# TensorE's attention batches as an engine loop, with the wait for the masked states ahead of the last head

## The chip, the cores and the metric

The kernel runs on one core of one Trainium2 chip. The time is the device time of one execution in microseconds; before the change it is 619.74 us, the median of three runs (619.48 to 620.28). Lower is better. Engines are named as in the profile: PE (TensorE), DVE (VectorE), ACT (ScalarE), POOL (GpSimd), SP (SyncE, which only issues transfers here).

## What is computed

A block of three sublayers on x of shape 8 x 512 x 128, all in float32:

```
x = x + 0.5 * ffn(layernorm(x))      # mixture of 64 experts, 6 per token, 64 slots each, and a shared expert
x = x + attention(layernorm(x))      # causal linear attention, 16 heads of 8
x = x + 0.5 * ffn(layernorm(x))

# attention, per batch and head, with feature map phi(z) = elu(z) + 1.0001:
q, k, v = split(x @ W_qkv + b_qkv);  q = phi(q / sqrt(8));  k = phi(k)
for t in range(512):
    kv += outer(k[t], v[t]);  ks += k[t]
    out[t] = (q[t] @ kv) / (q[t] . ks + 1e-6)
out @ W_out + b_out
```

## The kernel before

Each engine has one stream of instructions, written out by hand: the order in the source is the order of execution, and engines wait for each other with semaphores. The first feed-forward layer, the attention and the second feed-forward layer follow one another in every stream.

The attention goes batch by batch, one call of `step(b, par)` for each of the 8 batches; `par` is the parity of the batch and chooses between two buffers for q and v. The 512 tokens of a batch are cut into 4 groups q of 128, and these into 4 chunks of 32. Within a chunk, the scores are computed and masked; between chunks, a running state of key-value products is used. In PE's `step`:

- `project(b + 1)` (L835, L836, L838) computes q, k and v of the next batch: two matmuls with 512 columns and four with 128.
- `turn_out(b - 1)` (L856) transposes the output of the batch before.
- L880 is 64 score matmuls of 32 x 32 weights, in four groups of heads g. Between the groups come the state matmuls L899, 60 in all. After a wait for DVE's masking of a bank, the fourth group of states takes the first's bank again.
- `project_out(b - 1)` (L863) multiplies the transposed output by W_out.
- L913 is the score-value product: 16 heads h, 4 matmuls each. It waits for POOL's block-diagonal v (`vx_ready`) and for DVE's four masked scores (`sc_sb`, L1171).
- L926 is the product of q with the states, 60 matmuls. It waits for DVE's masked states (`kv_sb`, L1178) and their running sums (`sb_ready`, L1186). Its last one releases DVE's division (L1198) and POOL's L481 of the next batch (`o_ps`).
- `turn_k(b + 1)` (L848) transposes the next batch's k.

Each of these float32 products in L880, L899, L913, L926, L835, L836, L838 and L863 stands in the trace as two matmuls (128 for 64), each with a weight load (PEld); transposes stand as one. Waits are counts that grow with b, such as `PRIMED + NQ * (b + 1)`; no address depends on b beyond `par`.

DVE and POOL and, in its middle part, ACT already run their attention as loops of two steps (`Fori`), and their waits take values from a register. ACT's loop covers steps 1 to 4, DVE's steps 1 to 6. On PE the eight steps are written out: a Python loop emits steps 1 to 7 one after the other.

SP stores each batch's result and reads it back in another layout, when DVE has added the bias (L1159). The second feed-forward layer starts when that is back for the last batch.

Of the kernel before, what the change touches and what calls it, by code (L numbers as in the profile page):

```python
# [39 lines left out]
HEADS = 16  # L40
# [4 lines left out]
def macaron_kernel(nc, x, w_qkv, b_qkv, w_out, b_out, gate_wT, gate_b, w1T, w2T, w3T, ws1T, ws2T, ws3T, out):  # L45
    B, L, D = x.shape
# [9 lines left out]
    NQ = L // P  # L56
# [16 lines left out]
    with ctx:  # L73
# [3 lines left out]
        def sem(name):  # L77
            return ctx.enter_context(nc.semaphore(name))
# [155 lines left out]
        PRIMED = 1  # L234
# [18 lines left out]
        kv_sb = sem("kv_sb")  # L253
        sb_ready = sem("sb_ready")
# [413 lines left out]
        def _(pe):  # L668
# [158 lines left out]
            def project(b):  # L827

                pe.wait_ge(hTb_sb, b + 1)
                if not (isinstance(b, int) and b == 0):  # L830
                    pe.wait_ge(kv_sb, PRIMED + NQ * (b - 1))
                    pe.wait_ge(q_read, 2 * b)
                    pe.wait_ge(v_ready, b)
                    pe.wait_ge(k_read, 2 * b)
                pe.matmul(bank[0][:, :], wqkv[:, 0:D], HTB, start=True, stop=True).then_inc(qT_ps, 1)  # L835
                pe.matmul(bank[1][:, :], wqkv[:, D:2 * D], HTB, start=True, stop=True).then_inc(kT_ps, 1)  # L836
                for q in range(NQ):
                    ins = pe.matmul(bank[2][:, q * D:(q + 1) * D], HTB[:, q * P:(q + 1) * P], wqkv[:, 2 * D:3 * D],  # L838
                                    start=True, stop=True)
                ins.then_inc(v_ps, 1)  # L840

            def turn_k(b):

                if not (isinstance(b, int) and b == 0):
                    pe.wait_ge(oo_ready, PRIMED + b - 1)
                pe.wait_ge(k_ready, PRIMED + b + 1)
                for q in range(NQ):
                    ins = pe.transpose(bank[3][:, q * P:(q + 1) * P], KT[:, q * P:(q + 1) * P], ident[:, :])  # L848
                ins.then_inc(kn_ps, 1)

            def turn_out(b):
                if not (isinstance(b, int) and b == B - 1):
                    pe.wait_ge(kn_sb, PRIMED + NC * (b + 2))
                pe.wait_ge(an_ready, b + 1)
                for c in range(NC):
                    ins = pe.transpose(bank[3][:, c * P:(c + 1) * P], AN[:, c, :], ident[:, :])  # L856
                ins.then_inc(anT_ps, 1)

            def project_out(b):

                pe.wait_ge(anT_sb, b + 1)
                for c in range(NC):
                    ins = pe.matmul(bank[3][:, c * D:(c + 1) * D], AT[:, c * P:(c + 1) * P], wout[:, :],  # L863
                                    start=True, stop=True)
                ins.then_inc(pr_ps, 1)

            def step(b, par, first=False, last=False):
                if not last:
                    project(b + 1)
                pe.wait_ge(q4_ready, 4 * b + 4)  # L870
                pe.wait_ge(k_ready, PRIMED + b + 1)
                if not first:
                    turn_out(b - 1)

                for g in range(4):
                    rows = slice(32 * g, 32 * g + 32)
                    for q in range(NQ):
                        for c in range(NC):
                            t0 = q * P + c * CHUNK
                            ins = pe.matmul(bank[4 + g][CHUNK * c:CHUNK * c + CHUNK, q * P:(q + 1) * P]  # L880
                                            .rearrange("p (j t) -> p j t", j=4),
                                            KT[rows, t0:t0 + CHUNK], Q4[rows, :, t0:t0 + CHUNK],
                                            start=True, stop=True)
                    ins.then_inc(sc_ps, 1)

                    if g == 1:
                        pe.wait_ge(kn_sb, PRIMED + NC * (b + 1))
                        if last:
                            pe.wait_ge(v_ready, b + 1)
                        else:  # L890
                            pe.wait_ge(v_ready, b + 2)
                            pe.wait_ge(q_read, 2 * (b + 2))
                            pe.wait_ge(k_read, 2 * (b + 2))
                    for q in AFTER[g]:
                        if q >= len(STATES):
                            pe.wait_ge(kv_sb, PRIMED + NQ * b + q + 1 - len(STATES))
                        for c in range(NC if q < NQ - 1 else NC - 1):
                            for j in range(4):
                                ins = pe.matmul(bank[STATES[q % len(STATES)]][32 * j:32 * j + 32, c * GW:(c + 1) * GW],  # L899
                                                KN[:, c, q, 32 * j:32 * j + 32],  # L900
                                                VN[par][:, q, 4 * j:4 * j + 4, :].rearrange("p h f -> p (h f)"),
                                                start=True, stop=True)
                        ins.then_inc(kv_ps, 1)
                if not first:
                    project_out(b - 1)

                pe.wait_ge(vx_ready, PRIMED + NC * (b + 1))
                pe.wait_ge(sc_sb, 4 * b + 4)
                for h in range(HEADS):
                    ob = bank[4 + h // 4][:, 0:NC * GW].rearrange("p (c h f) -> p c h f", c=NC, h=4)  # L910
                    for q in range(NQ):
                        o = (h // 4) * L + q * P + (h % 4) * CHUNK
                        pe.matmul(ob[32 * q:32 * q + 32, :, h % 4, :], PR[:, o:o + CHUNK],  # L913
                                  VX[:, q, h, :, :], start=(h % 4 == 0), stop=False, skip_group_check=True)
                pe.wait_ge(kv_sb, PRIMED + NQ * (b + 1))
                pe.wait_ge(sb_ready, (NQ - 1) * (b + 1))
                for g in range(4):
                    rows = slice(32 * g, 32 * g + 32)
                    for c in range(NC):
                        for q in range(NQ):  # L920
                            if q + c == 0:
                                continue
                            t0 = q * P + c * CHUNK
                            before_c = SW[rows, q, c - 1, :] if c else SW[rows, q - 1, NC - 1, :]
                            o = c * GW
                            ins = pe.matmul(bank[4 + g][32 * q:32 * q + 32, o:o + GW], QT[par][rows, t0:t0 + CHUNK],  # L926
                                            before_c, start=False, stop=True, skip_group_check=True)
                ins.then_inc(o_ps, 1)
                if not last:
                    turn_k(b + 1)  # L930

            project(0)
            turn_k(0)
            step(0, 0, first=True)
            for b in range(1, B):
                step(b, b % 2, last=b == B - 1)
            turn_out(B - 1)
            project_out(B - 1)

# [315 lines left out]
```

## Time and profile before

| | |
|---|---|
| median of 3 runs | 619.74 us |
| the profiled execution | 623.67 us |
| its span, first to last instruction | 621.9 us |
| granted TensorE clock, mean | 0.698 |
| busy: PE, DVE, ACT, POOL | 441.1, 316.3, 237.2, 331.3 us |
| attention on PE, first projection to last | 236 to 396 us |
| steps 1 to 6 on PE | 264.6 to 372.6 us |

All times below come from the one profiled execution, 3.9 us above the median. A clock of 1.00 is 2.4 GHz, one of 0.50 is 1.2 GHz. "issue" as the releaser of a wait means that the profile shows nothing that the engine waited for: neither a semaphore of another engine nor a transfer. Idle time under 0.15 us is not listed as a wait. The queue whose kind is "instruction" carries the engines' own programs.

### The profile page before, as it was taken

Reading aid. Unit: us, or ns where it says so; the run is one execution under the profiler, and the core shown is the slowest. Engines: PE = TensorE matmul, PEld = TensorE weight load, DVE = VectorE, ACT = ScalarE, POOL = GpSimd, SP = SyncE. Lnnn points to the kernel's source line nnn. Section 1 sums busy time; section 2 is a strip of 40 time slices with the busy share of each in tenths; the row PEclk is TensorE's granted clock in tenths of the full one; section 3 lists DMA queues with packets and bytes.
Section 4 is the critical chain, followed back from the end, with each engine's and each line's share of the span. In section 5 each row is a group of like instructions: output and inputs, shape, how many; then the busy total and the mean of one; then the engine's idle time right before and its main releaser. Section 6 shows DMA issues by size and latency. Waiting matters only on the chain.

```text
span 621.9 us, 15104 instructions
## 1 busy us (share of the span) xinstructions
PE 441.1 (71%) x5988; PEld 291.9 (47%) x5988; DVE 316.3 (51%) x928; ACT 237.2 (38%) x629; POOL 331.3 (53%) x259
## 2 busy tenths in 40 slices
PE   1894957994798335798978988329757399947960
PEld 1842534552444322676767766229335255424440
DVE  6496952221107973454445564293999322212097
ACT  4961213331233387453534451168611133312420
POOL 6284776888887303022221222003886767888691
PEclk9986865555579556778779795656979655555995
DMA  8988401001029940001110110351000000000492
GB/s 270 380 254 339 180 3 12 5 7 9 4 78 405 408 194 1 3 3 37 37 38 22 38 38 20 92 230 69 1 1 8 6 9 6 9 7 7 157 410 110
DMA packets 34410, 60.74 MB, mean 98 GB/s; under 512 B 12611, under 2 KB 18846, under 8 KB 33870
## 3 DMA queue, kind: packets, MB, share of 16 engines
q1 hardware_dynamic: 23078, 58.41, 26.1%
q0 software_dynamic: 11264, 1.38, 2.4%
q8 instruction: 48, 0.79, 0.5%
q14 instruction: 20, 0.16, 0.1%
HBM read 37.43 MB, written 29.36 MB: 107 GB/s over the span
## 4 chain that ended last, share of the span: by engine, by line
PE 41%; DVE 27%; issue 12%; DMA 12%; ACT 4%; POOL 3%; SPq 1%; POOLq 0%; DVEq 0%; ACTq 0%
DVE X L977 8%; PE bank L780 6%; DMA rows_d<-A 5%; PE upper L797 5%; PE upper L880 5%; DVE Cb L1079 3%; ACT A L510 3%; PE upper L913 2%; PE bank L863 2%; DVE bn L982 2%; DMA Bb<-planes_d 2%; PE upper L926 2%; PE bank L899 2%; PE bank L835 2%; DMA A<-rows_d,tok_i 2%
## 5 line engine op out<-in xcount | busy, mean ns | idle before, releaser
L440 POOL DMA_INDIRECT planes_d<-Bb,put_i x64 | 100.4, 1569 | 26.4 <-issue 19.7
L454 POOL DMA_INDIRECT A<-rows_d,tok_i x64 | 71.9, 1124 | 20.6 <-issue 17.3
L1109 DVE TENSOR_TENSOR ring<-ring,bank 128x88 f32<-128x88 f32 x64 | 15.8, 246 | 107.1 <-ACT ring L578 71.1
L677 PE MATMUL bank<-ident,A 128*128 128x128 f32 x96 | 22.5, 413 | 53.9 <-ACT A L510 39.7
L481 POOL TENSOR_TENSOR Bb<-Cb,chm 128x576 f32<-128x576 f32 x16 | 19.0, 1220 | 76.3 <-PE upper L926 42.5
L481 POOL TENSOR_TENSOR Bb<-w3s,chm 128x576 f32<-128x576 f32 x16 | 17.8, 1147 | 56.2 <-PE upper L926 56.2
L398 POOL TENSOR_TENSOR Bb<-Eb,st 128x512 f32<-128x512 f32 x8 | 8.9, 1113 | 70.3 <-DVE st L1027 70.3
L677 PEld LDWEIGHTS bank<-ident,A 128*128 128x128 f32 x96 | 18.1, 220 | 57.1 <-issue 29.7
L797 PE MATMUL upper<-w2s,ring 88*64 88x128 f32 x256 | 44.0, 448 | 0.1
L1113 DVE TENSOR_SCALAR Bb<-upper,sl 128x128 f32<-128x128 f32 x64 | 22.5, 351 | 30.6 <-PE upper L797 24.5
L880 PE MATMUL upper<-A,Bb 32*32 32x128 f32 x1024 | 35.3, 296 | 2.1 <-issue 2.1
L780 PE MATMUL bank<-w1s,ring 128*64 128x88 f32 x256 | 35.7, 378 | 0.8 <-ACT ring L572 0.8
L423 POOL TENSOR_TENSOR PL<-PL 88x512 f32<-88x512 f32 x16 | 32.2, 2024 | 5.5 <-ACT PL L551 5.5
L631 ACT ACTIVATE w3s<-bank,upto 128x512 f32<-128x512 f32 x32 | 19.4, 688 | 40.3 <-PE bank L848 40.3
L977 DVE TENSOR_TENSOR X<-X,A 128x1024 f32<-128x1024 f32 x8 | 18.3, 2291 | 32.0 <-DMA Bb<-planes_d 32.0
L578 ACT ACTIVATE ring<-bank 128x88 f32<-128x88 f32 x64 | 15.5, 243 | 49.7 <-PE bank L780 26.5
L556 ACT ACTIVATE X<-upper 128x512 f32<-128x512 f32 x16 | 9.6, 597 | 65.3 <-PE upper L721 55.8
L780 PE MATMUL bank<-w3s,ring 128*64 128x88 f32 x256 | 32.4, 353 | 0.0
L770 PE MATMUL upper<-ident,A 128*128 128x128 f32 x32 | 15.0, 468 | 20.9 <-DMA A<-rows_d,tok_i 14.8
L880 PEld LDWEIGHTS upper<-A,Bb 32*32 32x32 f32 x1024 | 26.5, 114 | 5.8 <-issue 4.4
L510 ACT ACTIVATE A<-X,st 128x128 f32<-128x128 f32 x72 | 28.6, 480 | 0.0
L1171 DVE TENSOR_TENSOR A<-upper,causal 128x512 f32<-128x512 f32 x32 | 21.4, 687 | 12.3 <-PE upper L880 12.3
(179 smaller groups left out, 1098.0 us busy)
## 6 DMA issues: line engine op xcount, KB each, us to landing
planes_d<-zeros SPq DMA_DIRECT2D x8, 2048.0 KB, 20.6
w3s<-in_w3T SPq DMA_DIRECT2D x2, 2816.0 KB
rows_d<-A SPq DMA_DIRECT2D x8, 512.0 KB, 12.1
A<-planes_d SPq DMA_DIRECT2D x8, 512.0 KB, 9.3
PL<-planes_d SPq DMA_DIRECT2D x8, 512.0 KB, 10.0
Cb<-planes_d SPq DMA_DIRECT2D x8, 512.0 KB, 10.8
Bb<-planes_d SPq DMA_DIRECT2D x8, 512.0 KB, 11.9
w1s<-in_w1T SPq DMA_DIRECT2D x1, 2816.0 KB
```

The costliest lines, as they stand in the source:

```text
L423: pool.tensor_tensor(out=HS[g % 2][k], in0=SH[k], in1=H3[k], op=ALU.mult).then_inc(sh_gated, 1)
L440: pool.indirect_dma_start(out=planes_d[f], in_=Y[:, s, :], in_offset=None, out_offset=bass.IndirectOffsetOnAxis(ap=put_i[:, s:s + 1], axis=0),
L454: pool.indirect_dma_start(out=A[:, t, :], out_offset=None, in_=rows_d, in_offset=bass.IndirectOffsetOnAxis(ap=tok_i[:, t:t + 1], axis=0), ...
L481: pool.tensor_tensor(out=VX[:, :, :, c, :].rearrange("p q h f -> p (q h) f"), in0=VN[par].rearrange("p q h f -> p (q h) f"), in1=chm[:, c: ...
L510: ins = act.activation(A[:, i, :], X[:, i, :], ACT.Identity, bias=st[:, 1, i:i + 1], scale=st[:, 4, i:i + 1])
L677: ins = pe.transpose(bank[g % 2][:, (i % 4) * P:(i % 4 + 1) * P], A[:, i, :], ident[:, :])
L780: ins = pe.matmul(bank[2 + s % 2][CAP * k:CAP * k + CAP, off:off + I], XBT[s % 2][:, CAP * k:CAP * k + CAP], w[:, 2 * s + k, :], start=Tru ...
L797: ins = pe.matmul(bank[(4, 7)[s % 2]][CAP * k:CAP * k + CAP, 0:D], GT[s % 2][:, CAP * k:CAP * k + CAP], w2s[:, 2 * s + k, :], start=True, ...
L880: ins = pe.matmul(bank[4 + g][CHUNK * c:CHUNK * c + CHUNK, q * P:(q + 1) * P] .rearrange("p (j t) -> p j t", j=4), KT[rows, t0:t0 + CHUNK] ...
L977: then(dve.tensor_tensor(xg, xg, buf[:, cols], ALU.add))
L1113: dve.tensor_scalar(Y[:, s, :], bank[(4, 7)[s % 2]][:, 0:D], sl[:, 2, s:s + 1], 0.5, ALU.mult, ALU.mult).then_inc(y_sb, 1)
L1171: dve.tensor_tensor(PR[:, g * L:(g + 1) * L].rearrange("p (n t) -> p n t", t=CHUNK), bank[4 + g][:, :].rearrange("p (n t) -> p n t", t=CHUNK),
```

## The change

PE's steps 1 to 6 become an engine loop of three trips with two steps in its body, and step 7 follows it. In `step`, the two waits for DVE's masked states move from between L913 and L926 to ahead of the last of the 16 heads of L913. The matmuls and their order stay.

```
                 pe.wait_ge(vx_ready, PRIMED + NC * (b + 1))
                 pe.wait_ge(sc_sb, 4 * b + 4)
                 for h in range(HEADS):
+                    if h == HEADS - 1:
+                        pe.wait_ge(kv_sb, PRIMED + NQ * (b + 1))
+                        pe.wait_ge(sb_ready, (NQ - 1) * (b + 1))
                     ob = bank[4 + h // 4][:, 0:NC * GW].rearrange("p (c h f) -> p c h f", c=NC, h=4)
                     for q in range(NQ):
                         o = (h // 4) * L + q * P + (h % 4) * CHUNK
                         pe.matmul(ob[32 * q:32 * q + 32, :, h % 4, :], PR[:, o:o + CHUNK],
                                   VX[:, q, h, :, :], start=(h % 4 == 0), stop=False, skip_group_check=True)
-                pe.wait_ge(kv_sb, PRIMED + NQ * (b + 1))
-                pe.wait_ge(sb_ready, (NQ - 1) * (b + 1))
                 for g in range(4):
                     rows = slice(32 * g, 32 * g + 32)
                     for c in range(NC):
...
             project(0)
             turn_k(0)
             step(0, 0, first=True)
-            for b in range(1, B):
-                step(b, b % 2, last=b == B - 1)
+            with pe.Fori(0, (B - 2) // 2) as i:
+                step(2 * i + 1, 1)
+                step(2 * i + 2, 0)
+            step(B - 1, 1, last=True)
             turn_out(B - 1)
             project_out(B - 1)
```

## Rows read from the trace of the kernel before

**Rows 1.** The page's counts: busy us, share of the span, instructions.

```profile
PE 441.1 (71%) x5988; PEld 291.9 (47%) x5988; DVE 316.3 (51%) x928; ACT 237.2 (38%) x629; POOL 331.3 (53%) x259
...
q8 instruction: 48, 0.79, 0.5%
```

**Rows 2.** Windows: steps 1 to 6, step 2, step 6; busy us, instructions, clock, DMA.

```profile
264.60:372.60 108.00, 94.03 (x3150) 74.54 (x3145) 55.39 (x120) 49.47 (x83) 26.75 (x24) 0.81 0.12 31
284.90:303.70 18.80, 16.79 (x527) 13.34 (x525) 9.14 (x20) 8.29 (x14) 4.46 (x4) 0.75 0.14 32
357.10:372.60 15.50, 12.87 (x529) 10.22 (x525) 9.44 (x20) 7.78 (x13) 4.46 (x4) 1.00 0.15 38
```

**Rows 3.** The chain of work that ended last, 264.6 to 372.6 us, by line.

```profile
by line: PE upper L880 21.9%; issue 12.9%; PE upper L913 9.6%; PE bank L863 9.5%; PE bank L899 9.0%; PE upper L926 8.6%; PE bank L835 7.5%; PE bank L836 7.1%; PE bank L838 6.6%; PE bank L848 4.5%; PE bank L856 2.8%
```

**Rows 4.** PE's waits, 264.6 to 303.7, then 303.7 to 372.6: us, times, longest.

```profile
PE upper L926 <- issue: 3.4, 2, 2.1
PE upper L880 <- issue: 1.5, 2, 0.9
...
PE upper L926 <- issue: 6.9, 4, 2.1
PE bank L899 <- issue: 1.1, 1, 1.1
PE upper L880 <- issue: 0.5, 2, 0.3
```

**Rows 5.** PE's timeline at step 0's end: start us, us, what, idle before.

```profile
260.67 0.58 PE L913 MATMUL upper<-Bb,A 128*32 128x36 f32 x21 [1.77 <-issue]
261.18 1.55 PE L926 MATMUL upper<-Cb,Bb 32*32 32x36 f32 x107
264.22 0.45 PE L926 MATMUL upper<-Cb,Bb 32*32 32x36 f32 x13 [1.49 <-issue]
```

**Rows 6.** The DMA view, 264.6 to 372.6 us: packets, MB, share of 16 engines.

```profile
q8 instruction: 24, 0.39, 1.5%
```

**Rows 7.** PE's timeline, L926 in steps 1 and 2.

```profile
281.17 0.98 PE L926 MATMUL upper<-Cb,w3s 32*32 32x36 f32 x90
284.23 0.70 PE L926 MATMUL upper<-Cb,w3s 32*32 32x36 f32 x30 [2.08 <-issue]
...
300.69 1.06 PE L926 MATMUL upper<-Cb,Bb 32*32 32x36 f32 x74
303.11 0.61 PE L926 MATMUL upper<-Cb,Bb 32*32 32x36 f32 x46 [1.36 <-issue]
```

**Rows 8.** PE's timeline: L848 ahead of step 3, and the projection in steps 4, 5.

```profile
303.65 0.66 PE L848 MATMUL bank<-ident,Bb 128*128 128x128 f32 x4
...
323.70 1.91 PE L835 MATMUL bank<-Bb,wqkv 128*128 128x512 f32 x2
...
327.12 1.72 PE L838 MATMUL bank<-wqkv,Bb 128*128 128x128 f32 x8
...
341.03 1.02 PE L835 MATMUL bank<-Bb,wqkv 128*128 128x512 f32 x2
...
342.75 1.05 PE L838 MATMUL bank<-wqkv,Bb 128*128 128x128 f32 x8
```

**Rows 9.** ACT's timeline where its loop jumps back.

```profile
304.34 2.42 ACT L631 ACTIVATE w3s<-bank,upto 128x512 f32<-128x512 f32 x4 [5.58 <-PE bank L848]
306.63 0.70 ACT L614 ACTIVATE Eb<-bank,bq 128x512 f32<-128x512 f32 x1
```

**Rows 10.** DVE's timeline: last states of step 2 (in its loop) and step 7.

```profile
296.81 0.26 DVE L1178 TENSOR_TENSOR Cb<-bank,hm 128x108 f32<-128x108 f32 x1
297.19 0.27 DVE L1186 TENSOR_TENSOR Cb<-Cb 128x108 f32<-128x108 f32 x1
...
386.11 0.26 DVE L1178 TENSOR_TENSOR Cb<-bank,hm 128x108 f32<-128x108 f32 x1
386.41 0.27 DVE L1186 TENSOR_TENSOR Cb<-Cb 128x108 f32<-128x108 f32 x1
```

More of the change, by code:

```diff
@@ L909, in step @@
                 for h in range(HEADS):
+                    if h == HEADS - 1:
+                        pe.wait_ge(kv_sb, PRIMED + NQ * (b + 1))
+                        pe.wait_ge(sb_ready, (NQ - 1) * (b + 1))
                     ob = bank[4 + h // 4][:, 0:NC * GW].rearrange("p (c h f) -> p c h f", c=NC, h=4)
@@ L914, in step @@
                                   VX[:, q, h, :, :], start=(h % 4 == 0), stop=False, skip_group_check=True)
-                pe.wait_ge(kv_sb, PRIMED + NQ * (b + 1))
-                pe.wait_ge(sb_ready, (NQ - 1) * (b + 1))
                 for g in range(4):
@@ L934, in _ @@
             step(0, 0, first=True)
-            for b in range(1, B):
-                step(b, b % 2, last=b == B - 1)
+            with pe.Fori(0, (B - 2) // 2) as i:
+                step(2 * i + 1, 1)
+                step(2 * i + 2, 0)
+            step(B - 1, 1, last=True)
             turn_out(B - 1)
```

## Prediction

> **What bounds the kernel now.** I read the page's counts first, then windows over the attention steps, the chain, the waits of PE, and the timelines of PE, ACT and DVE where the edit falls. The change touches only attention. From 264.6 to 372.6 us run the six batch steps that become the loop, 18 us each on average, for instance 15.5 us at a granted clock of 1.00 and 18.8 at 0.75 [rows 2]. In these 108 us PE is busy 94, DVE 55, ACT 49, POOL 27. So PE bounds each step, and the chain through that stretch names PE's lines and "issue" and nothing else [rows 3]. There is no slack on another engine's side: any time that PE loses here moves the end.
>
> The idle time of PE in these six steps is put down to "issue" alone: 3.4 + 1.5 = 4.9 us in the first two steps, 6.9 + 1.1 + 0.5 = 8.5 us in the last four [rows 4]. What is it? The gaps come at a fixed distance. In step 0 matmuls resume at 260.67 and again at 264.22: between lie 21 + 107 = 128 matmuls, each with its weight load, so 256 instructions in 3.55 us [rows 5]. The queue of kind "instruction" moved 48 packets, 0.79 MB, over 2 x 5988 such instructions: 250 to a packet (some 256 with the waits), 16.4 KB each, and 24 of them in the six steps [rows 1, 6]. So PE's program comes in from memory in blocks of 256 instructions, four and a bit per step, and a block that is executed faster than the next arrives ends in a stall. The quick score-state matmuls of L926 are where that shows: stalls of 2.08 us after 90 of them in step 1, 1.36 after 74 in step 2 [rows 7]. The place moves back 16 or 17 matmuls a step, that is 33 instructions, so a step is four blocks and 33 instructions long: 1057. The 3.55 us is what one block costs from the moment that the one before it is entered to its first matmul; one block is asked for ahead, no more, or these stalls would not be there at all.
>
> **The change part by part.**
>
> Straight-line code becomes a body of two steps: 2 x 1057 = 2114 instructions and some 20 of register work, 8.3 blocks, run three times. No matmul, DMA or other engine's instruction is added or removed, and no queue but PE's is touched. The fetching is not saved, if blocks are read in order: about as many blocks are passed as before.
>
> (a) Two jumps back, after steps 2 and 4. The target lies 8 blocks behind. By [rows 5] a fetch takes 3.55 us; the block ahead of the branch is in, the target is not. What PE has queued covers little: before step 3 the stall in L926 ends at 303.11, 46 of its matmuls and the 4 transposes of L848 follow and end at 304.31 [rows 7, 8]; the issuing side stands perhaps 0.3 us ahead of that, estimated from 46 matmuls in 0.61 us. So 3.3 us net each, 6.6 us. Bounds: nothing, if a jump is as free as ACT's own back-edge in this place (ACT's loop jumps between the four L631 copies, which take from 304.34 to 306.76, and L614, which starts at 306.63 without a gap [rows 9], though that body is short); above, the target's fetch might wait for the ahead-fetch of a now useless block, entered at 303.11: 3.55 + about 3.2 = 6.8 us each, 13.6 us. I take 3.3 because it is the same fetch on the same engine.
>
> The Trainium skill ("Runtime: NRT & Kernel Launch", Instruction fetch mechanics) says that a taken branch to a page outside a two-page window has to fetch it before going on. That rule would give the same sum as the 3.3 us term.
>
> (b) Register work. In the loop a wait's value is computed. DVE shows the price: from the start of L1178 to that of L1186 it is 0.38 us in its loop and 0.30 in its written-out last step, 0.08 us for one update [rows 10]. PE has 21 waits a step by the source. All of them exposed would be 6 x 21 x 0.08 = 10 us; none exposed, 0. Those near the long matmuls of L835 to L863 are issued while PE works off its queue, and those inside L880 mostly too. I count the two of the last head, where small matmuls run as fast as they are issued: 6 x 2 x 0.08 = 1.0 us.
>
> (c) The moved waits. They now hold back the last head's 4 products (8 of 128 matmuls, 0.13 us) as well as L926. In step 2 DVE's last state, L1186, ends at 297.46; L926 starts at 300.69 [rows 10, 7]. 3.2 us of L863 and L913 hide it: cost 0. If that cover were gone, 0.13 us a step, and DVE's last mask would be late next.
>
> (d) Clock. A step at a granted 1.00 took 15.5 us, one at 0.75 took 18.8 [rows 2]. After a pause the long project matmuls run first: from the start of L835 to the end of L838 they took 5.1 us at the low level of 1.2 GHz (323.70 to 328.84) and 2.8 at the high one of 2.4 (341.03 to 343.80) [rows 8], 2.3 us apart. Before step 3 they already ran partly low; before step 5 they ran high and would lose it. Between 0 and 2 x 2.3 = 4.6 us; I take about half of one such loss, 1.2 us, as a pause of this length may or may not cost the level.
>
> (e) Stall places. Iterations 2 and 3 repeat the block places of steps 1 and 2: 2 x 4.9 = 9.8 us instead of 8.5. The steps at a high clock stall differently, so I take half, 0.6 us (bounds 0 and 1.3).
>
> Sum: 6.6 + 1.0 + 0 + 1.2 + 0.6 = 9.4 us. The profiled execution took 623.67 us (span 621.9), 3.9 above the median of 619.74, so it becomes 633.1, and the median 629.1.
>
> **The rivals.**
>
> *Both fetches in line (slower still).* If the target's fetch waits for the one already under way, (a) is 13.6: sum 16.4, 636.1 us. For it: one packet at a time is all that the trace ever shows. Against: nothing shows a queue that refuses a second.
>
> *The body stays resident (faster).* If PE kept the blocks it has passed, iterations 2 and 3 would fetch nothing, and the 8.5 us of stalls after 303.7 us would go, with jumps free: -8.5 + 1.0 = -7.5, 612.2 us. It decides from the point where the kept blocks number as many as the body's, 9 by their edges; with fewer kept and the oldest dropped, each is gone before it is wanted. For it: nothing in this trace, where PE never goes back. Against: with room for so many, one block ahead would be a strange economy.
>
> The Trainium skill ("Advanced Engine Details and Errata", ISA Cache) gives TensorE 128 KB, which would be 8 such blocks, but also only two cache lines. By the first the body would miss by a fraction of a block, by the second by far; both leave this rival small.
>
> *Nothing that can be told (same).* The jump's target comes in under cover or the compiler arms a fetch for it, and only the register work stays: +1.0, 620.7 us. Against: nothing in the source asks for that. That the loop does not do what it says is no separate case: three trips of two steps are steps 1 to 6, and the waits keep their values.
>
> **How the numbers follow.** Forecast 0.70, both in line 0.13, resident 0.10, nothing 0.07. What a measurement here can tell from no change is 0.2%, 1.2 us. Faster 0.10, same 0.07, slower 0.83. The forecast's own range is 624 (fetch 2.5 us net, the rest near nothing) to 635 (register work and clock at more than double). Taking in the slower rival gives 623.5 to 638, with 0.83 of the chance before its edges.
>
> **What would show it.** PE gaps of 3 to 4 us marked "issue" before L835, twice, about 40 us apart, and none before the first body; still about 24 instruction packets or more in the stretch; L926 stalls after about the same two counts of matmuls in every iteration; L926 no later behind L913. Instruction packets falling to 8 or so in the stretch would prove residence, and gaps of 6 us the queued fetch. The forecast is wrong if PE's gap before L835 is under 1 us, or if PE's small matmuls L899 and L913 slow down throughout, which would be the register work at its upper bound.

## The result, and the profile after

The changed kernel takes 643.73 us in the median of 4 runs (642.94 to 644.94), the kernel before 620.01 us (619.48 to 623.0): a ratio of 1.0374, 95% interval 1.0337 to 1.0411. It is slower by 24 us, outside the stated range of 623.5 to 638. Its profiled execution took 643.94 us with a span of 642.2, which is 20.3 us more than the span before; the profile before was of a run 3.7 us above its median, which is the rest.

The branch back, by source line of the changed kernel: the entry of PE's sequencer, times in ns as least/median/most.

```profile
L936 PEldq COMPARE_BRANCH  x3: 76/4513/4634, 302.7 to 390.5; - x3
```

Two branches are taken and take 4.5 and 4.6 us, the third falls through in 0.08. The instruction queue from the start of the first branch to its end (302.7 to 307.2 us), and over all six steps (before: 24 packets [rows 6]):

```profile
q8 instruction: 2, 0.03, 4.4%
...
q8 instruction: 28, 0.46, 1.6%
```

The two packets of the first line start at 303.16 and 303.74 us: the block ahead, asked for when the last block was entered, and the branch's target. They overlap, and the second takes 2.06 us (2.15 at the other jump), where the other packets of this queue from 260 to 395 us take 0.9 to 1.6. PE's waits in the same six steps, now 264.2 to 390.5 us, and then in what follows up to 415 us:

```profile
PE upper L927 <- issue: 13.0, 6, 2.5
PE bank L835 <- issue: 8.3, 2, 4.4
PE upper L880 <- issue: 4.5, 6, 1.1
...
PE bank L856 <- ACT w3s L631: 2.7, 1, 2.7
PE upper L927 <- issue: 1.9, 1, 1.9
```

Against [rows 4] (6.9 + 3.4 at this line, which was L926, and 1.5 + 0.5 + 1.1 at L880 and L899, 13.4 in all) there are 8.3 us of a new kind, and 17.5 of the old one, 4.1 more; a stall of 1.9 us has come to step 7 too, where the kernel before had none. The windows: all six steps, then steps 2 to 6. A wait for a branch lies in the windows of steps 3 and 5 alone.

```profile
264.20:390.50 126.30, 100.55 (x3149) 77.66 (x3144) 54.64 (x120) 50.03 (x83) 26.75 (x24) 0.74 0.11 27
283.10:302.60 19.50, 17.01 (x531) 13.08 (x524) 9.15 (x20) 8.30 (x14) 4.46 (x4) 0.74 0.12 31
302.60:326.10 23.50, 16.08 (x537) 12.27 (x525) 9.10 (x20) 8.51 (x14) 4.46 (x4) 0.75 0.11 27
326.10:346.60 20.50, 16.94 (x528) 13.15 (x524) 9.14 (x20) 8.41 (x14) 4.46 (x4) 0.75 0.12 29
346.60:370.20 23.60, 16.70 (x531) 12.69 (x524) 9.10 (x20) 8.51 (x14) 4.46 (x4) 0.72 0.12 26
370.20:390.50 20.30, 17.11 (x530) 13.39 (x524) 9.14 (x20) 7.89 (x13) 4.46 (x4) 0.75 0.12 29
```

The number of matmuls is that of [rows 2], but PE is busy 100.5 us with them instead of 94.0 and the granted clock is 0.74 instead of 0.81. Step 6, 15.5 us at a clock of 1.00 before, takes 20.3 at 0.75, with no jump in it. So of the 18.3 us that the six steps grew, 8.3 are the jumps, 4.1 longer stalls and some 6 the slower matmuls, which fits the lower clock. The last is the surprise. The timeline at the first jump:

```profile
299.39 1.11 PE L927 MATMUL upper<-Cb,Bb 32*32 32x36 f32 x68
302.06 0.65 PE L927 MATMUL upper<-Cb,Bb 32*32 32x36 f32 x52 [1.56 <-issue]
302.64 0.66 PE L848 MATMUL bank<-ident,Bb 128*128 128x128 f32 x4
307.67 2.05 PE L835 MATMUL bank<-Bb,wqkv 128*128 128x512 f32 x2 [4.37 <-issue]
```

And the stall of L927 comes after 68 matmuls in every even step and after 87 in every odd one, where in straight line it moved back 16 or 17 a step [rows 7].

### The profile page after: what moved, and what is told of

It reads as the page before. It is cut to its first block, busy times and chain, and to the rows that moved or that the text cites. A ratio compares the mean times of both kernels' runs of the same rounds, so it can differ in the third digit from the quotient of the medians.

```text
span 642.2 us, 15141 instructions
## 1 busy us (share of the span) xinstructions
PE 446.7 (70%) x5988; PEld 293.7 (46%) x5988; DVE 315.9 (49%) x928; ACT 238.2 (37%) x629; POOL 331.5 (52%) x259
## 4 chain that ended last, share of the span: by engine, by line
PE 40%; DVE 25%; issue 14%; DMA 12%; ACT 4%; POOL 3%; SPq 1%; POOLq 0%; another core or an unknown queue 0%; DVEq 0%; ACTq 0%
DVE X L980 8%; PE bank L780 6%; DMA rows_d<-A 5%; PE upper L880 5%; PE upper L797 4%; DVE Cb L1082 3%; ACT A L510 2%; PE bank L863 2%; PE bank L835 2%; PE upper L916 2%; DVE bn L985 2%; DMA Bb<-planes_d 2%; POOL planes_d L440 2%; PE upper L927 2%; PE bank L836 2%
## 5 line engine op out<-in xcount | busy, mean ns | idle before, releaser
L481 POOL TENSOR_TENSOR Bb<-w3s,chm 128x576 f32<-128x576 f32 x16 | 17.8, 1146 | 64.4 <-PE upper L927 64.4
L880 PE MATMUL upper<-A,Bb 32*32 32x128 f32 x1024 | 35.1, 291 | 4.5 <-issue 4.5
L980 DVE TENSOR_TENSOR X<-X,A 128x1024 f32<-128x1024 f32 x8 | 20.8, 2596 | 33.1 <-DMA Bb<-planes_d 33.1
L578 ACT ACTIVATE ring<-bank 128x88 f32<-128x88 f32 x64 | 15.5, 243 | 45.5 <-PE bank L780 27.3
L880 PEld LDWEIGHTS upper<-A,Bb 32*32 32x32 f32 x1024 | 25.9, 112 | 8.5 <-issue 7.1
L770 PE MATMUL upper<-ident,A 128*128 128x128 f32 x32 | 14.9, 465 | 20.3 <-DMA A<-rows_d,tok_i 14.3
```

Of the source, the lines that this page charges most:

```text
L481: pool.tensor_tensor(out=VX[:, :, :, c, :].rearrange("p q h f -> p (q h) f"), in0=VN[par].rearrange("p q h f -> p (q h) f"), in1=chm[:, c: ...
L980: then(dve.tensor_tensor(xg, xg, buf[:, cols], ALU.add))
```

## The experiments

Ratios are against the kernel before, measured beside each variant on the same chip; its own median went from 616 to 625 us from one set of runs to another, so only ratios are compared. Where a time per step is given, it comes from one profiled execution. "Place" is where in its fetch block of 256 instructions a step's first instruction stands, counted in the program and fixed by the stalls: step k of the straight-line kernel stands at 34 + 33 (k - 1).

**The moved waits alone.** Straight line, with the two waits ahead of the last head.

```
-            with pe.Fori(0, (B - 2) // 2) as i:
-                step(2 * i + 1, 1)
-                step(2 * i + 2, 0)
-            step(B - 1, 1, last=True)
+            for b in range(1, B):
+                step(b, b % 2, last=b == B - 1)
```

> Straight-line batches as before, with the two waits for the masked states ahead of the last head. Both theories: no difference to before (within 0.2%), since the last state is masked 3 us earlier. A difference over 1.2 us would mean that the place of the waits has a price of its own.

0.9985 (0.9953 to 1.0018). They cost nothing that can be told. The other half alone, the loop with the waits in their old place, was not run.

**A hint for the branch.**

```
-            with pe.Fori(0, (B - 2) // 2) as i:
+            with nc.Fori(0, (B - 2) // 2, engines=[mybir.EngineType.PE], hint_back_edge=True) as i:
```

> The changed kernel, with a branch prefetch hint at the head of the loop's body and nothing else. Theory J (the jumps and what their pauses do to the clock make the cost): the two 4 us gaps before L835 shrink to under 1 us, steps 4 to 6 get the high clock back, and the time falls by 14 us or more, to 620 to 630 us. Theory B (the body costs by itself: register values at the waits, and block edges that fall in the same place each time): the gaps shrink, but only their 8 us come back: 635 us.

1.0285 (1.019 to 1.0381), which is not clear of the changed kernel's own 1.0374 and, repeated below, 1.0301. Both theories were wrong about the gap: the branch still takes 3.0 us. The third line is the instruction queue during the first branch (305.4 to 308.4 us).

```profile
L936 PEldq BRANCH_PREFETCH_HINT  x3: 31/40/45, 265.8 to 348.9; - x3
...
L936 PEldq COMPARE_BRANCH  x3: 80/2977/3035, 305.4 to 386.7; - x3
...
q8 instruction: 1, 0.02, 2.2%
```

The stall in L927 just before ends at 304.7, the branch at 305.4 + 3.0 = 308.4: 3.7 us, about a block's fetch. There is one packet instead of two. It starts at 305.78, 1.05 us after the stall's end (1.1 at the other jump), as the packets of the block ahead do. So the hinted fetch is asked for on entering the block with the branch, in place of the block ahead, and this block holds only some 118 instructions ahead of it.

**The pauses without loop or branch.** The straight-line kernel; before the projection of steps 3 and 5 PE waits for POOL.

```
+                if b in (3, 5):
+                    pe.wait_ge(vx_ready, PRIMED + NC * (b + 1))
                 if not last:
                     project(b + 1)
```

> Straight-line batches as before, with a pause of PE put before the projection of steps 3 and 5, where the loop jumps back (it waits there for POOL's block-diagonal v of its own batch, due some 4 us after L926). No register value, no jump. Theory J: as slow as the changed kernel or nearly, 636 to 643 us, with the clock lower in the steps behind each pause. Theory B: only the two pauses are paid, 627 to 629 us.

1.0163 (1.0082 to 1.0244), 10.2 us. PE's waits in its steps 1 to 6 and the head of step 7:

```profile
PE upper L928 <- issue: 9.0, 6, 2.3
PE bank L835 <- POOL Bb L481: 8.2, 2, 4.1
```

8.2 us of pauses, as long as the changed kernel's and in the same places, cost 10 us (5 to 15 by the interval); in the profile the six steps take 117.9 us, 9.9 more than before. PE is busy 97.2 us in them instead of 94.0, about half of what the changed kernel's matmuls lost (100.5), and the other stalls, 12.5 us for 13.4, give some of it back. The two pauses explain about half of the loss, 10.2 of 20 to 24 us.

**One jump instead of two.**

```
-            with pe.Fori(0, (B - 2) // 2) as i:
+            with pe.Fori(0, 2) as i:
                 step(2 * i + 1, 1)
                 step(2 * i + 2, 0)
-            step(B - 1, 1, last=True)
+            for b in range(5, B):
+                step(b, b % 2, last=b == B - 1)
```

> The loop takes two trips (steps 1 to 4), steps 5 to 7 are written out: one jump back instead of two. Theory J: one gap of about 4.4 us before step 3's L835, none before step 5's; about half of the 24 us, 630 to 633 us. Theory B: the body is run in two of three pairs of steps, so about two thirds of its share of 15 and one jump: 634 us.

1.0211 (1.0125 to 1.0297), one gap of 4.3 us. The difference of the two expectations was too small to be told. But steps 5 and 6, out of the loop, take 17.6 and 17.0 us, where the loop needed some 20 each beside its jump: the body is slow also where it does not jump. (They do not stand where the straight-line kernel has them, but behind the body, at 118 and 151 by the same count.) Beside the jumps and the 2 us that the pauses cost beyond their length, something in the body costs 10 us by the profiles, 13 by the medians.

**Where the body stands in its block.** Register values at the waits (theory R) or the places of the block edges (theory P)? The loop can be moved:

```
-            with pe.Fori(0, (B - 2) // 2) as i:
+            with nc.Fori(0, (B - 2) // 2, engines=[mybir.EngineType.PE], head_slot={mybir.EngineType.PE: 166}) as i:
```

> The changed kernel once more, beside the three others of this call. Both theories: 1.03 to 1.04 of before, so 643 to 650 us against whatever before takes on this chip.

> The changed kernel with the loop's body placed so that its first instruction stands at place 166 of a fetch block of 256, where the straight-line code of the kernel before has its step 5; in the changed kernel it stands at 36, as step 1 did. Same instructions, same two jumps back. Theory P (the body is slow since block edges fall at steps 1 and 2's places in every trip, which were the slow ones): a trip without its jump takes 34 to 36 us instead of 39, and the time falls by 6 to 12 us. Theory R (register values at the waits make the body slow): no change, within 2 us.

> As the one before, with a branch prefetch hint as well. The branch back then stands near place 250 of its block, so that a fetch asked for on entering that block has the block's whole time. Both theories: the gap before L835 falls from 4.4 us to under 1 us (with the branch at place 118 the hint only brought it to 3.1), 7 to 9 us faster than the same placing without the hint. With P: within 5 us of the kernel before, or faster than it. With R: about 10 us slower than before.

> The changed kernel with its body at place 100 of a fetch block instead of 36; 166 gave 1.007, 36 gave 1.030. Theory P (the place of the block edges makes a trip slow or fast): between the two or near 166, 1.01 to 1.02, with other stall places but again the same ones in every trip. Theory R (register values): 166 was an exception, and this one is back at 1.03.

The unchanged loop gave 1.0301 (1.0226 to 1.0376), at place 100 it gave 1.019 (1.0123 to 1.0257), at 166 1.0071 (1.0034 to 1.0108). The instructions are the same and so are the two jumps back (moving the body adds one short jump ahead of it, 0.32 us): 0.023 of the whole, 14 us, lie in the place. The two intervals of 36 and 166 are apart; that of 100 overlaps with 36's. The profile of place 166, PE's waits from 263.9 to 374.3 us and windows of its three trips:

```profile
PE upper L927 <- issue: 8.5, 6, 2.2
PE bank L835 <- issue: 7.3, 2, 4.1
PE upper L880 <- issue: 1.1, 3, 0.5
```

```profile
264.00:299.40 35.40, 32.25 (x1049) 25.50 (x1048) 18.16 (x40) 16.71 (x28) 8.91 (x8) 0.74 0.11 27
299.40:336.60 37.20, 30.90 (x1052) 23.61 (x1051) 18.25 (x41) 16.81 (x28) 8.91 (x8) 0.80 0.13 32
336.60:374.20 37.60, 30.17 (x1049) 23.23 (x1048) 18.08 (x41) 16.41 (x27) 8.91 (x8) 0.82 0.14 33
```

The stalls fell from 17.5 to 9.6 us beside the jumps, and the clock is up. Windows of the kernel before, its steps 1, 3, 4 and 5 (2 and 6 are in [rows 2]):

```profile
264.60:284.90 20.30, 17.33 (x530) 13.63 (x525) 9.02 (x20) 8.40 (x14) 4.46 (x4) 0.75 0.07 16
303.70:322.80 19.10, 15.94 (x527) 12.66 (x525) 9.20 (x20) 8.29 (x14) 4.46 (x4) 0.79 0.12 31
322.80:340.50 17.70, 15.46 (x527) 12.00 (x524) 9.08 (x20) 8.41 (x14) 4.46 (x4) 0.84 0.14 33
340.50:357.10 16.60, 15.63 (x537) 12.70 (x525) 9.52 (x20) 8.29 (x14) 4.46 (x4) 0.79 0.14 36
```

The second and third trip of the loop, from L848 to L848 and less the gap at L835 (at place 36 4.37 and 3.95 us, at 100 4.25 and 4.27, at 166 3.19 and 4.11), beside two straight-line steps at the same places; the last column has the same steps in the two other straight-line profiles, of the moved waits alone and of the copies below:

| body's place | trip in the loop, mean of two | kernel before | steps there | two other profiles |
|---|---|---|---|---|
| 36 | 39.8 us, repeated 38.7 | 39.0 us | 1 and 2 | 39.0, 37.9 us |
| 100 | 36.7 us | 36.9 us | 3 and 4 | 37.2, 38.9 us |
| 166 | 33.7 us | 32.0 us | 5 and 6 | 33.6, 33.7 us |

Place 166 is the fast one in all of them, in the loop and out of it. Between 36 and 100 the order is less sure: 100 took 38.9 us once. With the hint at place 166 the time was 1.0085 (1.0044 to 1.0127), no better than without, against what I expected: the branches still took 2.6 and 2.2 us. In place 166 PE stalls in L927 just on entering the last block and then runs its 242 instructions in 1.6 us (297.7 to 299.3 in the run without the hint), so a fetch of 3.6 us finds less cover than I had counted. The gaps fell from 7.3 to 4.1 us all the same, but the trips took 35.5 us instead of 33.7, with 12.0 us of other stalls instead of 9.6; why is open.

**The same shift without a loop.**

```
+            for k in range(66):
+                pe.transpose(bank[3][0:32, 0:32], ident[0:32, 0:32], ident[0:32, 0:32])
             for g in range(NSH):
                 xT(1, g)
```

> The kernel before with 66 small transposes (132 instructions) put ahead of attention where PE idles, so that its step 1 stands at place 166 and each following step 33 further, round the block. No loop. Theory P: steps 1 and 2 get faster, as steps 5 and 6 were, the later ones pass through other places; the sum over six steps changes by a few us at most, 0.99 to 1.01 of before. If a step's speed did not follow its place, the steps keep their old times one by one: 20, 18, 19, 17, 16.5, 15.5 us.

Steps 1 and 2 now stand at 166 and 199, in windows from L850 (before, L848) to L850:

```profile
264.60:281.60 17.00, 14.51 (x527) 11.26 (x524) 9.11 (x20) 8.30 (x14) 4.46 (x4) 0.89 0.08 18
281.60:297.10 15.50, 13.98 (x535) 10.67 (x525) 9.06 (x20) 8.31 (x14) 4.46 (x4) 0.89 0.14 35
```

17.0 and 15.5 us; in the kernel before steps 1 and 2 took 20.3 and 18.8, while steps 5 and 6, at these places there, took 16.5 and 15.5. Steps 3 to 6, at places 232, 9, 42 and 75:

```profile
297.10:316.00 18.90, 15.72 (x530) 12.81 (x525) 9.62 (x20) 8.30 (x14) 4.46 (x4) 0.82 0.14 35
316.00:335.10 19.10, 16.05 (x526) 12.56 (x525) 9.24 (x20) 8.30 (x14) 4.46 (x4) 0.78 0.13 31
335.10:353.70 18.60, 16.51 (x526) 12.84 (x525) 9.03 (x20) 8.33 (x14) 4.46 (x4) 0.77 0.12 32
353.70:373.10 19.40, 17.08 (x530) 13.40 (x524) 9.15 (x20) 7.79 (x13) 4.46 (x4) 0.74 0.12 30
```

A step's speed follows its place, not its number. All six take 108.5 us, 0.5 more than before, as expected. The whole is 1.0064 (1.0025 to 1.0103), 4 us: most of it lies behind the six steps, where the code has moved within its blocks too. Step 7, now at place 108, has a stall of 0.85 us in L928 that it did not have; the rest was not followed up.

**How much of a loop PE keeps.** Loops of 32 x 32 transposes ahead of all work, three trips each, in two kernels.

```
+            for n in (50, 200, 540, 1060):     # the other kernel: (750, 890, 950, 1010)
+                with pe.Fori(0, 3) as i:
+                    for k in range(n):
+                        pe.transpose(bank[3][0:32, 0:32], ident[0:32, 0:32], ident[0:32, 0:32])
```

> The kernel before, with four loops of small transposes put ahead of all its PE work, three trips each, bodies of 100, 400, 1080 and 2120 instructions; only the branches and the gaps behind them are read. If PE keeps only a window of two blocks: the branch of the 100-instruction body takes 0.3 us, that of 400 instructions 0.3 or 4 by where it lies, those of 1080 and 2120 about 4 to 4.5 us in every trip, and stalls inside these bodies are alike in all trips. If it keeps eight blocks: 1080 instructions jump in 0.3 us, without stalls in the second and third trip, and only 2120 misses.

> The probe with bodies of 1500, 1780, 1900 and 2020 instructions, three trips each. If PE keeps eight blocks of 256 and drops the oldest, a body is kept as long as its blocks by their edges, and perhaps the one fetched ahead, number eight at most: 1500 (7 at most) jumps in 0.2 us with no packets in trips 2 and 3, 2020 (9 by its edges) misses with 3.4 us, and 1780 and 1900 fall on either side by where they lie. If the limit is lower, 1500 misses too; if the 2130 of the changed kernel's body missed for another reason than its size, all four jump in 0.2 us.

| instructions | branches back, us | instruction packets in trips 1, 2, 3 |
|---|---|---|
| 100 | 0.23, 0.21 | 0, 0, 0 |
| 400 | 0.23, 0.21 | 1, 1, 0 |
| 1080 | 0.21, 0.21 | 4, 0, 0 |
| 1500 | 0.25, 0.21 | 6, 0, 0 |
| 1780 | 4.4, 4.5 | 7, 8, 9 |
| 1900 | 3.5, 3.7 | 8, 9, 9 |
| 2020 | 3.3, 3.8 | 8, 10, 10 |
| 2120 | 3.4, 3.5 | 8, 10, 10 |

The branches of the first kernel, and the DMA view of its third loop's first trip (41.4 to 70.2 us), whose second and third trip (to 127.7 us) have no such row:

```profile
L672 PEldq COMPARE_BRANCH  x12: 76/208/3484, 3.6 to 302.6; - x12
```

```profile
q8 instruction: 4, 0.07, 0.9%
```

PE does keep blocks that it has passed. 1500 instructions stay, 1780 don't. Eight blocks with one of them fetched ahead would fit that (1780 instructions touch up to eight by their edges), but no run fixes the number. The changed kernel's body, some 2130, would have to lose a sixth or more of its instructions.

**A body that stays.** One step as the body needs q and v of every batch in one place. DVE copies them there.

```
-            with pe.Fori(0, (B - 2) // 2) as i:
-                step(2 * i + 1, 1)
-                step(2 * i + 2, 0)
+            with pe.Fori(1, B - 1) as b:
+                step(b, 0)
...
+            def keep_v(b, par):
+                dve.wait_ge(v_ready, b + 1)
+                dve.wait_ge(kv_ps, PRIMED + NQ * b)
+                dve.tensor_copy(VNS[:, :], VN[par].rearrange("p q h f -> p (q h f)")).then_inc(vs_ready, 1)
...
+            def keep_q(b, par):
+                dve.wait_ge(q_ready, PRIMED + b + 1)
+                dve.wait_ge(o_ps, PRIMED + b)
+                dve.tensor_copy(QTS[:, :], QT[par]).then_inc(qs_ready, 1)
```

In PE's step L899 reads `VNS` and L926 `QTS`, with a wait for each.

> PE's loop with one step in its body, about 1080 instructions, six trips. PE reads q and v of every batch from one place, into which DVE copies them (two copies a batch, in DVE's idle time). Theory K (PE keeps about eight blocks, as the probe's body of 1080 instructions showed; the changed kernel's body of 2130 misses by a fraction of a block): the branch back takes 0.2 us, instruction packets stop after the first trip, the issue gaps in trips 2 to 6 are gone with some 10 us, the clock rises, and it beats both kernels: 0.97 to 0.985 of before. Theory W (only a window of two blocks counts in real code): gaps as before and five more branches of 4 us, 1.03 of before or worse.

> The control for the run before: the same two DVE copies a batch and the same waits, but PE's batches written out in straight line. Both theories: within 0.5% of the kernel before, as the copies lie in DVE's idle time; whatever it differs by is the copies' share in the run before.

0.9667 (0.9604 to 0.973): 603.35 us beside 625.09. The copies in straight line: 0.9983 (0.9942 to 1.0025), so they have no part in it that can be told. The branches of the loop, the instruction packets of its trips 2 to 6 (286.3 to 350.9 us), and windows of all six steps and of the third trip (L933 is L926's and L852 L848's line here):

```profile
L942 PEldq COMPARE_BRANCH  x6: 76/212/240, 286.3 to 350.9; - x6
...
q8 instruction: 1, 0.02, 0.1%
```

```profile
266.80:350.90 84.10, 80.88 (x3150) 64.78 (x3145) 64.34 (x132) 49.42 (x83) 27.87 (x24) 0.92 0.13 32
300.20:312.90 12.70, 12.56 (x537) 10.17 (x525) 10.76 (x22) 8.31 (x14) 4.65 (x4) 1.00 0.18 43
```

```profile
311.73 1.23 PE L933 MATMUL upper<-Cb,w3s 32*32 32x36 f32 x120
312.89 0.66 PE L852 MATMUL bank<-ident,Bb 128*128 128x128 f32 x4
```

The six steps take 84.1 us, against 108.0 [rows 2] and 126.3. The first trip is as slow as ever (19.5 us), the second takes 13.9; from the third on each takes 12.65 us at the full clock, all 120 matmuls of L926 pass in one piece, and PE is busy 12.56 of 12.7 us with register values at its waits. It beats both kernels.

## Why the prediction was wrong

Direction and engine were right, and so was the mechanism of the jumps: PE bounds the steps, its program is fetched in blocks, the target of the jump is not there, and the two gaps before L835 show as foretold, 44 us apart. The profile grew by 20.3 us where 9.4 were forecast. Term by term:

- **Step (a), the jumps.** 3.3 us net each was taken, 4.37 and 3.95 measured; 8.3 us for 6.6. The branch takes 4.5 us (5.0 in the repeat), more than the 3.55 of a block fetched in order: its packet took 2.06 and 2.15 us beside that of the block ahead. In place 166, where the packet of the first jump had no other beside it, it took 1.45 us and the branch 3.9. So the rival of two fetches in line (6.8 each) had the useless block right and the queue wrong: the two run side by side, and the branch is about 1 us longer for it and not 3.
- **Step (b), register work.** 1.0 us was taken and up to 10 allowed. With register values in every step, the resident body leaves PE at most 0.14 us idle in a step of 12.7, 0.8 us or less for six.
- **Step (c), the moved waits.** Nothing, as said.
- **Step (e), the places of the stalls. This is the step that failed.** I saw that the loop would repeat the places of steps 1 and 2 and counted only the stalls themselves, halved: 0.6 us. Straight line passes through six places, the last two faster by some 2 to 5 us a step than the first two; the loop stays in two slow ones. The six steps less their two gaps took 118.0 us for the 107.9 of straight line, 10 us more. Three times the 39.0 us of steps 1 and 2 make 117, which the profile of before already held, had I set step times against places instead of stalls against stalls. With those 9 us for 0.6 the sum would have been 17.8 and the median 637.5, inside the range; the first measurement gave 643.73, and the ratio of the repeat, 1.0301, would make it 638.4.
- **Step (d), the clock.** 1.2 us was taken for the pauses; the pauses alone cost about 2 us beyond their length, with 3.1 us more of busy time for the same matmuls. The changed kernel had 6.5 us more. The rest goes with the places; that stalls which come again in each step keep the clock from rising, as it did in steps 3 to 6 of before (0.79, 0.84, 0.79, 1.00, against 0.72 to 0.75 here), is the likely way and not shown. In the sum (d) and (e) had 1.8 us for 10 in the six steps. The prediction took the fast late steps as a matter of the clock alone; the shifted kernel shows that they go with the place.
- Step 7's new stall, 1.9 us, was not in the sum. It too fits a place: the code after the loop stands at 118 instead of 232, and the shifted kernel, whose step 7 stands at 108, has a stall of 0.85 us there.

The resident rival got 0.10 and did not come, but its mechanism is real, and my argument against it ("a strange economy") was wrong: one block is fetched ahead, and yet several passed ones are kept. The Trainium skill ("Runtime: NRT & Kernel Launch", Instruction fetch mechanics) calls it a window of two pages; the probe's 1080 and 1500 instructions, jumped back over in 0.2 us with no packets, speak against that here. The Trainium skill ("Advanced Engine Details and Errata", ISA Cache) gives TensorE 128 KB in lines of 16 KB, which is eight blocks, and in the same list only two lines. 1500 kept speaks for the first and against the second; 1780 lost is less than the 2048 instructions of eight blocks, and agrees with them only if one block is taken by the fetch ahead.

What stays open: how a place turns into a speed, in numbers. The stalls at places 36 and 166 differ by 8 us over six steps, the clock does the rest, but nothing here forces a given clock, so the two are not told apart. Place 166 in the loop is 1.7 us a trip slower than in the kernel before, but not slower than in the two other straight-line profiles (33.6 and 33.7 us).

## What to carry to other kernels

Count the instructions of a loop's body on TensorE, both records of every matmul included. A body that is kept (1080 here in the kernel, 1500 in the probe) has no instruction stalls after its first trip; to halve the body for that was worth two small copies on another engine. One that is just too long (1780 and up) pays 3.3 to 5.0 us for each jump and fetches everything again. Where dense small matmuls outrun the fetch, the place of the block edges has a price of its own: moving the same loop within its block was worth 14 us here, and 66 small transposes put where PE idles made the whole slower by 0.6 per cent. So an edit anywhere ahead in the stream can shift the time, and a difference of that size is no proof of what the edit was meant to do.

## What the runs showed of the hardware that was not expected

- The attention's straight-line matmul stream is held up by its fetch (3.55 us for 256 instructions); freed of that, a step of attention went from 15.5 to 20.3 us down to 12.65.
- PE keeps code that it has passed: 1500 instructions were jumped back over in 0.2 us, 1780 were fetched again in every trip.
- Two instruction packets can be under way at once, and then the second takes longer: 2.1 us instead of 0.9 to 1.6.
- A prefetch hint at the head of the body took only 1.5 us off a branch of 4.5, since its packet starts 1.05 us after the block with the branch is entered and no earlier.
- Two pauses of 8.2 us together cost 10.2 (5 to 15 by the interval).
